# Causal attention on one core: projections as pairs of 64 columns in three PSUM banks, a new order of the unit, and 3 of 16 transfers issued by ScalarE

## The reference

```python
def _L0_attn_ref(x, qkv_w, qkv_b, out_w, out_b):        # x: (4, 1024, 128)
    qkv = jnp.einsum('bse,ehd->bshd', x, qkv_w) + qkv_b
    q, k, v = jnp.split(qkv, 3, axis=-1)
    logits = jnp.einsum('bqhd,bkhd->bhqk', q, k)
    logits = logits / jnp.sqrt(jnp.asarray(q.shape[-1], logits.dtype))
    mask = jnp.tril(jnp.ones((q.shape[1], q.shape[1]), dtype=jnp.bool_))
    logits = jnp.where(mask, logits, _large_negative_number(logits.dtype))
    probs = jax.nn.softmax(logits, axis=-1)
    attn = jnp.einsum('bhqk,bkhd->bqhd', probs, v)
    return jnp.einsum('bqhd,hde->bqe', attn, out_w) + out_b
...
x = x + _L0_attn_ref(xn, ...) + _L0_ffn_ref(xn, ...)     # layer 0
xn = _layernorm(x)
x = x + _L1_attn_ref(xn, ...) + _L1_ffn_ref(xn, ...)     # layer 1: fast weights, 8 experts
```

## Time and profile before

| | |
|---|---|
| time, median of 3 runs | 1467.65 us (1464.54 to 1470.5) |
| time of the profiled execution | 1468.25 us |
| its span, first to last instruction | 1466.5 us |
| mean granted TensorE clock | 0.997 |
| PE busy | 1414.2 us (96%) |
| DVE busy | 1254.1 us (86%) |
| POOL busy | 970.4 us (66%) |
| ACT busy | 917.8 us (63%) |
| attention of layer 0, unit 0 to unit 31 | from 64.93 us to about 920 us |

### The profile page before, as it was taken

One profiled execution on the slowest core, in us unless ns is written; L12 is line 12 of the kernel. 1 busy time (PEld: TensorE's weight loads), 2 busy tenths in 40 slices (PEclk: granted clock), 3 DMA queues, 4 the chain that ended last, 5 costly groups with the idle time before them and its releaser, 6 DMA issues.

```text
span 1466.5 us, 27229 instructions
## 1 busy us (share of the span) xinstructions
PE 1414.2 (96%) x9282; PEld 905.1 (62%) x9282; DVE 1254.1 (86%) x1966; ACT 917.8 (63%) x1862; POOL 970.4 (66%) x756
## 2 busy tenths in 40 slices
PE   8989999999999999999999998789999999999998
PEld 7756555555565565655655555456667676776767
DVE  7588888888888888888888877399999999999997
ACT  3456666766676666666666675557665675657552
POOL 5145545546555556555556554559999999999895
PEclk9999999999999999999999999999999999999999
DMA  8058777877787777777787778300000000000000
GB/s 191 1 130 213 180 175 174 194 169 177 174 190 182 173 176 187 172 185 178 180 190 170 171 182 202 86 1 1 1 8 8 1 8 1 8 8 1 8 1 15
DMA packets 77140, 163.98 MB, mean 112 GB/s; under 512 B 31410, under 2 KB 43724, under 8 KB 77004
## 3 DMA queue, kind: packets, MB, share of 16 engines
q1 hardware_dynamic: 77004, 162.24, 46.5%
HBM read 9.08 MB, written 2.10 MB: 8 GB/s over the span
## 4 chain that ended last, share of the span: by engine, by line
PE 83%; DVE 7%; issue 4%; POOL 3%; ACT 2%; DVEq 0%; ACTq 0%; POOLq 0%
PE accum L1096 18%; PE both L1031 13%; PE misc L998 9%; PE both L2786 8%; PE flips_all L1031 6%; PE flips_all L2809 4%; PE flips_all L1120 4%; PE misc L1008 4%; PE flips_all L2798 3%; PE flips_all L2846 2%; PE accum L2798 2%; PE accum L2809 2%; PE flips_all L2832 1%; ACT big L534 1%; PE flips_all L969 1%
## 5 line engine op out<-in xcount | busy, mean ns | idle before, releaser
L453 POOL TENSOR_SCALAR big<-big,recip 128x384 f32<-128x384 f32 (+7 forms) x512 | 376.1, 749 | 414.8 <-DVE recip L705 414.8
L713 DVE STREAM_TRANSPOSE big<-big 128x896 f32<-128x896 f32 (+7 forms) x288 | 346.0, 1228 | 17.5 <-POOL big L453 17.2
L534 ACT ACTIVATE big<-both,neg_max 128x1024 f32<-128x1024 f32 (+3 forms) x256 | 243.3, 956 | 169.0 <-DVE neg_max L695 160.5
L1096 PE MATMUL accum<-across,v_sb 128*64 128x256 f32 (+1 forms) x2560 | 271.6, 363 | 11.0 <-issue 10.9
L1096 PEld LDWEIGHTS accum<-across,v_sb 128*64 128x64 f32 x2560 | 178.8, 137 | 132.7 <-issue 68.9
L695 DVE TENSOR_REDUCE neg_max<-both 128x1 f32<-128x1024 f32 (+3 forms) x256 | 248.3, 1011 | 7.8 <-PE both L1036 7.8
L1031 PE MATMUL both<-qk_sb 64*128 64x512 f32 (+3 forms) x1024 | 212.9, 532 | 12.5 <-issue 8.6
L2786 PE MATMUL both<-slow_sb,h_T 128*128 128x512 f32 x384 | 181.1, 599 | 7.9 <-DVE xnT L2299 4.4
L1595 POOL TENSOR_TENSOR prod<-xnT,qs 128x1024 f32<-128x1024 f32 (+3 forms) x32 | 180.2, 5635 | 11.1 <-DVE qs L2299 11.1
L534 ACT ACTIVATE big<-flips_all,neg_max 128x128 f32<-128x128 f32 (+3 forms) x256 | 131.9, 526 | 83.3 <-DVE neg_max L695 46.9
L1031 PEld LDWEIGHTS both<-qk_sb 64*128 64x128 f32 x1024 | 93.9, 186 | 117.5 <-issue 117.5
(11 more groups left out here) (224 smaller groups left out, 2403.7 us busy)
## 6 DMA issues: line engine op xcount, KB each, us to landing
across<-big SPq DMA_DIRECT2D x1024, 144.0 KB, 2.5
out<-x SPq DMA_DIRECT2D x8, 256.0 KB, 2.3
x<-in_L_attn_x SPq DMA_DIRECT2D x3, 512.0 KB, 5.6
slow_sb<-in_L_attn_w_slow SPq DMA_DIRECT2D x3, 512.0 KB, 7.2
w_qk<-in_L_attn_qkv_w SPq DMA_DIRECT2D x2, 512.0 KB, 6.5
xn<-in_L_ffn_W SPq DMA_DIRECT2D x1, 1024.0 KB
x<-in_L_attn_x SPq DMA_DIRECT2D x2, 256.0 KB, 3.0
qs<-in_L_attn_qkv_w SPq DMA_DIRECT2D x1, 512.0 KB, 6.1
```

What stands on the lines that cost most here:

```text
L453: pool.tensor_scalar(part, part, recip[:, u % 2, SLOTS.index(row), h:h + 1], 0.0, ALU.mult, ALU.add).then_inc(scaled, 1)
L534: last = act.activation(probs_of(row, h).rearrange("p b j k -> p j b k"), scores_of(row, h).rearrange("p (j b k) -> p j b k", b=MOVES, k=3 ...
L713: dve.transpose(part, part).then_inc(turned[group_of(row)], 1)
L1096: last = pe.matmul(dst, lhsT=values_of(u, j, h), rhs=keys_of(g, rows[n:n + 2], j, h), start=j == 0, stop=j == rows[n + 1])
```

## The change

- `project`, `project_values` and `join` write their 128 output partitions as two matmuls of 64 stationary columns each (h = 0, 1), one to each half of the array's columns, with the same moving data.
- The projections of a unit take all three banks: (1, 0) and values 1 bank 0, (0, 0) bank 1, the others bank 2. Units 0 and the flips at the end stay in bank 2 (`FIRST`).
- ACT issues the last 3 of the 16 DMAs of each group (`move_rest`), SP the first 13 (`OWN`), but for the last unit, where SP issues all. SP's pass u is now `move(u - 1, 0)`, `move(u - 1, 1)`.
- `weigh` takes parts (pair of rows, from, to), so a group is weighed in other portions.
- PE, DVE, ACT and POOL have new orders of the unit. On DVE the turns of rows 3, 2 and 4 stand in the next pass, ahead of row 7's maxima, and the maxima of row 5 stand ahead of the turns of rows 1, 6 and 0.
- The tail into layer 1 follows these orders.

```diff
+LAST_LOW = 0, 0
-BANK = {('v', 0): 2, ('qk', 0, 1): 2, ('qk', 1, 0): 2, ('qk', 0, 0): 2, ('qk', 1, 1): 2, ('o', 0): 0, ('o', 1): 1, ('v', 1): 2}
+BANK = {('qk', 1, 0): 0, ('qk', 0, 1): 2, ('v', 1): 0, ('qk', 1, 1): 2, ('qk', 0, 0): 1, ('v', 0): 2, ('o', 0): 0, ('o', 1): 1}
+FIRST = ('v', 0), ('qk', 0, 1), ('qk', 1, 0), ('qk', 0, 0), ('qk', 1, 1), ('v', 1)
+BLOCKS = [(a, a ^ k) for k in range(MOVES) for a in (0, 2, 1, 3)]
+OWN = 13
...
         @block.sync   (move)
-                for k in range(MOVES):
-                    for a in (0, 2, 1, 3):
-                        b = a ^ k
-                        sp.dma_start(across[g][32 * b:32 * (b + 1), a, :], runs[g][32 * a:32 * (a + 1), b, :]).then_inc(moved[g], 16)
+                for a, b in BLOCKS[:OWN if u < UNITS - 1 else len(BLOCKS)]:
+                    sp.dma_start(across[g][32 * b:32 * (b + 1), a, :], runs[g][32 * a:32 * (a + 1), b, :]).then_inc(moved[g], 16)
...
+                move(u - 1, 0)
                 move(u - 1, 1)
-                move(u, 0)
...
         @block.gpsimd   (unit)
                 scale(u, 7, 0)
-                scale(u, 0, 1)
+                scale(u, 7, 1)
                 scale(u, 1, 0)
-                scale(u, 7, 1)
-                scale(u, 0, 0)
-                scale(u, 1, 1)
-                scale(u, 6, 0)
                 scale(u, 6, 1)
...
+                scale(u, 1, 1)
+                scale(u, 0, 0)
+                scale(u, 6, 0)
+                scale(u, 0, 1)
...
         @block.scalar
+            def move_rest(u, g):
+                if not 0 <= u < UNITS - 1:
+                    return
+                act.wait_ge(turned[g], TURNS[g] * (u + 1))
+                if u:
+                    act.wait_ge(weighed, weighed_at(u - 1, "high", g))
+                else:
+                    act.wait_ge(branch_ready, 2 * B)
+                for a, b in BLOCKS[OWN:]:
+                    act.dma_start(across[g][32 * b:32 * (b + 1), a, :], runs[g][32 * a:32 * (a + 1), b, :]).then_inc(moved[g], 16)
...
             def unit(u):
+                keep_part(u + 1, 1, 0)
                 softmax(u, 7, 1)
                 softmax(u, 7, 0)
                 if UNITS - B <= u < UNITS - 1:
                     first_norms(u - (UNITS - B))
+                move_rest(u - 1, 1)
+                softmax(u, 1, 1)
+                softmax(u, 1, 0)
                 softmax(u, 0, 1)
                 softmax(u, 0, 0)
-                softmax(u, 1, 1)
-                softmax(u, 1, 0)
-                keep_values(u + 1, 0)
+                softmax(u, 6, 1)
                 softmax(u, 6, 0)
                 keep_part(u + 1, 0, 1)
-                softmax(u, 6, 1)
-                keep_part(u + 1, 1, 0)
                 keep_att(u - 1, 0)
+                softmax(u, 2, 0)
                 softmax(u, 2, 1)
-                softmax(u, 2, 0)
+                softmax(u, 5, 1)
+                keep_values(u + 1, 1)
                 softmax(u, 5, 0)
-                softmax(u, 5, 1)
+                keep_part(u + 1, 1, 1)
+                softmax(u, 3, 0)
+                softmax(u, 3, 1)
+                softmax(u, 4, 0)
+                softmax(u, 4, 1)
                 keep_part(u + 1, 0, 0)
                 keep_att(u - 1, 1)
-                softmax(u, 3, 0)
-                softmax(u, 3, 1)
-                keep_part(u + 1, 1, 1)
-                softmax(u, 4, 0)
-                softmax(u, 4, 1)
-                keep_values(u + 1, 1)
                 keep_join(u - 1, 0)
+                move_rest(u, 0)
+                keep_values(u + 1, 0)
                 keep_join(u - 1, 1)
...
         @block.vector   (unit)
+                turn(u - 2, 3)
+                turn(u - 2, 2)
+                turn(u - 2, 4)
                 maximum(u - 1, 7, 1)
                 maximum(u - 1, 7, 0)
-                maximum(u - 1, 0)
                 maximum(u - 1, 1)
                 invert(u - 1, 0)
-                invert(u - 1, 4)
+                maximum(u - 1, 0)
+                maximum(u - 1, 6, 1)
                 maximum(u - 1, 6, 0)
-                maximum(u - 1, 6, 1)
...
                 turn(u - 1, 7)
                 invert(u - 1, 1)
+                invert(u - 1, 4)
                 maximum(u - 1, 2)
-                turn(u - 1, 0)
-                turn(u - 1, 1)
-                turn(u - 1, 6, 0)
-                turn(u - 1, 6, 1)
-                invert(u - 1, 6)
+                maximum(u - 1, 5, 1)
                 maximum(u - 1, 5, 0)
-                maximum(u - 1, 5, 1)
...
-                turn(u - 1, 2)
+                turn(u - 1, 1)
+                turn(u - 1, 6, 1)
+                turn(u - 1, 6, 0)
+                turn(u - 1, 0)
                 invert(u - 1, 2)
                 maximum(u - 1, 3)
+                invert(u - 1, 6)
...
                 turn(u - 1, 5)
                 invert(u - 1, 3)
-                turn(u - 1, 3)
-                turn(u - 1, 4)
...
         @block.tensor   (project; project_values and join in the same way)
-                pe.matmul(pool_of[k], lhsT=w_qk[:, c, P * n:P * (n + 1)], rhs=xnT[:, u // PAIRS, 512 * half:512 * (half + 1)],
-                          start=True, stop=True).then_inc(bank_made[k], 1)
+                for h in range(2):
+                    at = P * n + D * h
+                    last = pe.matmul(pool_of[k][D * h:D * (h + 1), :], lhsT=w_qk[:, c, at:at + D],
+                                     rhs=xnT[:, u // PAIRS, 512 * half:512 * (half + 1)], start=True, stop=True)
+                last.then_inc(bank_made[k], 1)
...
             def unit(u):
                 score(u, 0)
+                project(u + 1, 1, 0)
+                project(u + 1, 0, 1)
+                weigh(u - 1, 0, (0, 0, 2), (2, 0, 2))
                 score_small(u, 4)
-                project_values(u + 1, 0)
-                weigh(u - 1, 0, 0, 4)
                 score(u, 1)
+                weigh(u - 1, 0, (2, 2, 8))
                 score_small(u, 6)
-                project(u + 1, 0, 1)
-                weigh(u - 1, 0, 4, 8)
-                project(u + 1, 1, 0)
                 score(u, 2)
-                project(u + 1, 0, 0)
-                weigh(u - 1, 1, 0, 4)
-                weigh(u - 1, 1, 4, 6)
+                weigh(u - 1, 1, (0, 0, 4))
+                project_values(u + 1, 1)
+                project(u + 1, 1, 1)
                 score_small(u, 5)
                 score(u, 3)
-                project(u + 1, 1, 1)
+                weigh(u - 1, 1, (2, 0, 6))
+                project(u + 1, 0, 0)
+                project_values(u + 1, 0)
                 join(u - 1, 0)
                 join(u - 1, 1)
-                project_values(u + 1, 1)
```

More of the change, by code:

```diff
@@ L122, with __init__ @@
 GROUPS = (0, 1)
-EARLY = (('qk', 0, 1), ('qk', 1, 0))
+EARLY = (('qk', 1, 0), ('qk', 1, 1))
 class Tally:
[L128 to L132, removed]
+    def __init__(self, order, head=None, tail=None, over=()):
+        self.at, n = {}, 0
+        for body in range(-1, UNITS + 2):
+            if body == -1 and head is not None:
+                keys = [(key, 1) for key in head]
+            elif body >= UNITS and tail is not None:
+                keys = [(key, -1) for key in tail]
+            else:
+                keys = order
+            for key, ahead in keys:
+                if 0 <= body + ahead < UNITS:
                     n += 1
                     self.at[(body + ahead,) + key] = n
-        self.met = 0
+            for key in over if body == UNITS - 1 else ():
+                n += 1
+                self.at[(UNITS,) + key] = n
+        self.met, self.total = 0, n
     def __call__(self, u, *key):
@@ L208, in layer0 @@
                 ((0,), -1), ((1,), -1),
-            ])
+            ], tail=((0,), (1,)))
     tails = {}
@@ L1007, in project_values @@
                 for r in range(2):
-                    last = pe.matmul(pool_of[k][:, 256 * r:256 * (r + 1)], lhsT=xnT[:, b, P * (2 * c + r):P * (2 * c + r + 1)],
-                                     rhs=w_v[:, P * n:P * (n + 2)], start=True, stop=True)
+                    for h in range(2):
+                        at = P * (2 * c + r) + D * h
+                        last = pe.matmul(pool_of[k][D * h:D * (h + 1), 256 * r:256 * (r + 1)], lhsT=xnT[:, b, at:at + D],
+                                         rhs=w_v[:, P * n:P * (n + 2)], start=True, stop=True)
                 last.then_inc(bank_made[k], 1)
@@ L1079, in has_values, with weigh @@
                     pe.wait_ge(bank_kept[k], use)
[L1081 removed]
+            def weigh(u, g, *parts):
                 if done(u):
@@ L1088, in weigh @@
                     has_values(u, 0)
-                if hi > GB:
+                if parts[-1][2] > GB:
                     has_values(u, 1)
-                for n in range(0, GB, 2):
-                    for j in range(lo, min(hi, rows[n + 1] + 1)):
+                for n, lo, hi in parts:
+                    for j in range(lo, hi):
```

(8 more changed lines are left out.)

86 lines of the change are left out of this document (43 added, 43 removed).

## The result

The changed kernel takes 1553.53 us (median of 4 runs, 1550.79 to 1554.86) beside 1467.48 for the kernel before: a ratio of 1.0581, with a 95% interval from 1.0559 to 1.0602. The forecast was 1443.5 us with a range up to 1472; the time is 82 us beyond that end. The profiled execution has a span of 1553.1 us beside 1466.5.

What follows compares the result with a forecast made beforehand. PE bound the kernel at 26.61 us a unit; the loop over group 0 would set 25.65. Thirty units save 28.8 us, the last pays 4.3: 1468.25 becomes 1443.7, stated as 1443.5; own range 1433 to 1457, wider range 1425 to 1472.

Steps and rivals of the forecast that it cites:

- D = 11.25: Time in us from a group being turned to its copies' landing, foretold down from a mean of 12.5.
- part 2: ACT issues 3 of a group's 16 transfers: shorter landing, for 3.8 us of ACT's time a unit.
- both bounds of the split: Landing time 10.55 us if DMA engines take two trains at once (chance 0.18), about 12.0 if they are full (0.12).
- SP's train of 13: SP's 13 issues of a group were to take 8.3 us; stretching trains at DMA share 0.96 would show the forecast wrong.
- The slower rival: ACT's late issues queue behind SP's train, landing stays 12.5 us: 1481 us; with the case of costlier ACT issues, chance 0.15.
- The loop over group 0: Rows 0, 1, 6, 7: maxima and turns 10.0 us, landing, then weighing and scores 4.4; 25.65 us, setting the unit.
- PE's work: Per unit, 26.04 us falls to 25.1 through the pairs of 64 columns; bounds 25.0 and 26.0.
- A change of shape: Each change of PE's tile shape costs 0.19 us; four fewer a unit save 0.76 us.
- ACT's issues: Each issue costs ACT 0.64 us, 3.8 us a unit; at 1.3 us each a unit would take 27.3.
- wait ahead of row 5's scores: PE waits 0.1 to 0.2 us there for row 6's exponentials; this wait would show ACT's issues as the cause.
- POOL's 14.4 us: GpSimd's scaling and adding in a unit, taken only to follow the other engines.
- The last unit: Group 0 of unit 30 goes out behind W2 and b2; costs 4.3 us on the path into layer 1.

Runs made afterwards that it cites:

- a_early0: The changed kernel, with ACT issuing group 0's last three copies ahead of row 3's exponentials instead of behind the output projection's copy: 1505.42 us, ratio 1.0266.
- a_sp16: The changed kernel, but SP issues all 16 copies of a group and ACT none: 1529.88 us, ratio 1.0403.
- b_pairs: The kernel before with only the pairs of 64 columns in project, project_values and join; orders, banks and DMAs as before: 1466.9 us, ratio 0.9982.
- a_dev_w2: The changed kernel, with second_deviation behind group 0's scalings on POOL and unit 30's group 0 sent before W2 and b2: 1530.2 us, ratio 1.0414.
- b_pairs_act4: The kernel before in its own order, with the pairs and ACT issuing 4 of a group's 16 copies: 1479.19 us, ratio 1.0066.
- a_max5: The changed kernel, but DVE takes row 5's maxima behind the turns of rows 1, 6 and 0: 1629.25 us, ratio 1.1094.

## Why the prediction was wrong

**The step that failed** is D = 11.25 in part 2, the time from the turned group to its landing. It measured 13.65 and 12.66 us in the units shown and 13.2 on the mean. The prediction named both bounds of the split, 10.55 and 12.0, and chose a point near the lower one "since a landing only 1.94 us behind the last issue leaves no room for a pile of transfers". The half-size copies refute that reason: with the same issues and half the bytes D fell to 10.7, so the bytes held the landing, and no pile showed before since the issues came no faster than the copies drained. The copies of one group are 16 x 147,456 bytes, 10.3 us at the 228 GB/s of the earlier trace rows, and SP's train of 16 took 10.25: the two limits coincided before, so a train's shape couldn't tell which one held. The DMA share of 0.96 in the earlier trace rows could, and I discounted it. The Trainium skill ("DMA: Bandwidth & Descriptors", "Issuing engines are not separate DMA queues") says that a second issuer saves sequencer time alone; the runs agree: where both issue, the engines move 211 GB/s, and 242 in a train of SP's alone (windows in the last section), and in the order of before the split shortened D by 0.3 us. SP's train of 13 takes 9.4 us on the mean of the units, not 8.3: the prediction's own sign of being wrong.

**Why D became even longer than before.** The slower rival had part of the mechanism: ACT comes to group 0's three issues only when SP's train is nearly over. The timeline has them 6.3 us behind SP's first, and a_early0 shows their place to be worth 48 us. The rival took D = 12.5, as if late issues merely saved nothing; a_sp16, with the same order and SP alone, has 12.8, so 0.4 of the 13.2 are the late issues'. The other 0.4 over the 12.4 of before are there without ACT, in longer trains of SP (10.9 us beside 10.4); why they are longer stays open. That late issues cost time fits an overlap of the two trains: group 1's first copy, issued at 532.21, lands at 535.61, ahead of group 0's last, which is SP's own thirteenth (issued at 530.30, landed at 536.08). In the ten of 29 units where a copy of group 1 is ahead like that D is 13.6 on the mean, and 13.0 in the others. So the overlap is at most a part, and it is argued from the timeline; no run kept group 1's train back.

**Right in mechanism, nearly in size.** The loop over group 0, 14.4 + D, measured 14.5 + D. PE's work, 25.1 foretold, is 25.4 in the chain of the kernel after and 25.3 with the waits gone: inside the bounds, but 0.6 to 0.7 us saved and not 0.94. A change of shape costs 0.15 us in these rows, not 0.19. In the chain of the kernel after `project` and `project_values` take 0.86 beside others and 1.01 behind scores, and the output projection 1.75 instead of 1.97. The saving existed; at D = 13 nobody could use it. ACT's issues take 0.63 us each (three in 1.88), as assumed, and no wait ahead of row 5's scores appeared.

**Terms that the sum lacked.** `second_deviation` in the loop over group 0: I had read POOL's 14.4 us as following, and priced no instruction that the diff moved among its scalings. The last unit costs 11.9 us and not 4.3. Of the 7.6 us between, 2.8 are the later first issue (964.18 - 935.35 = 28.8, not 26.0, as the unit ahead is longer), 2.2 are D twice (12.6 and 13.4, not 11.25 and 12.5), and 2.5 PE's slow restart behind the wait. The loop over group 1 got no sum: in the kernel before it already took 26.3 us (13.8 from landing to first issue at the least, and 12.4), as long as PE's own work, which is what b_pairs ran into. And PE's granted clock, below.

**The sums.** With D = 13.2 the loop, 14.6 us from landing to first issue by the trace, gives 27.8 a unit, 30 x 1.2 = 36 of the 69.9 us lost. The trace divides the rest. From group 0's landing to the next first issue 15 of 30 units take 14.6 us. Eight take 16.2: there PE's clock fell behind the wait, 13 us in all. The six around the three ends of batches take 16.1 to 19.9, 21 us in all. The thirtieth, 21.5, belongs to the last unit above. The price of the change without the split, 60 us in a_sp16, is the largest single item. By the same count 24 of them are its D (14.6 + 12.8 = 27.4 a unit); the deviation and the last unit were shown in a_dev_w2 (23 us together), the maxima in the loop were not, and how much each is of the 60 was not measured.

## What to carry to other kernels

When a train of transfers is as long as its issues and also as long as its bytes at the measured rate, take the DMA share inside the train as the verdict: at 0.96, a second issuer took 0.3 us off 12.4 at best. Before an order spends the cover of a loop, price the loop at the measured latency and not at a hoped-for one: this order needed D under 12.3 us to break even by the prediction's own sum, and D had been 12.5. If transfers are shared out over two engines, those of the second must be early in the train, and nothing urgent may stand behind them: at its end they made D longer (13.2 beside 12.8 without them), and a fourth one, early, cost PE 18 us of waits.

## What the runs showed of the hardware

An issue of SP takes 0.59 us in the median of the kernel before, but single ones stretch to 1.97, and they do so with SP alone at work: 19 of some 1020 take over 1.2 us there. The 1.57 us of b_pairs_act4 stand at 504.52, 3 us before ACT's first issue. One such row of the kernel before, at a DMA share of 0.49:

```profile
494.91 1.53 SPq L355 DMA_DIRECT2D across<-big  x1
```

What stretches these is not shown. Beside that, issues of two engines that overlap are slower: in the kernel after those of SP that overlap one of ACT take 0.77 us on the mean, with half of the bytes 0.69, where SP alone in the kernel before has 0.61. The rate doesn't rise with two issuers. Windows of the kernel after, inside a train of SP's alone and where both issue (last: clock, DMA share, GB/s):

```profile
524.00:526.00 2.00, 2.00 (x24) 1.42 (x22) 1.94 (x4) 2.00 (x7) 2.00 (x4) 1.00 1.03 242
529.00:531.00 2.00, 2.00 (x20) 1.12 (x18) 1.58 (x2) 0.61 (x2) 1.27 (x1) 1.00 0.93 211
```

A wait of PE can be paid for twice. Behind the wait of 2.72 us the 16 records of the weighing took 1.73 us; behind one of 3.56 us they took 3.26, and the granted clock falls in that stretch. The length of the wait alone doesn't decide it: behind 2.19 us they took 2.45 (clock 0.75 from 506.50 to 508.00), and behind 2.83 us, at 157.76, they took 1.73 at the full clock. What decides it these rows don't tell.

```profile
97.64 3.56 issue
101.19 3.26 PE accum L1124 x16
...
504.19 2.19 issue
506.39 2.45 PE accum L1124 x16
```
```profile
358.00:366.00 8.00, 5.14 (x38) 3.18 (x40) 0.69 (x3) 2.30 (x4) 0.00 (x0) 0.79 1.00 237
```

The last row is the same event in unit 10, behind a wait of 3.57 us: a mean clock of 0.79 between full, 2.4 GHz, and half, 1.2 GHz. Over the stretch of all units the granted clock is 0.98 where it was 1.00, so of the 896 us at most some 2%, 18 us (an estimate from the two clocks), is lost that way; the eight loops of 16.2 us instead of 14.6 are 13 of them. In a_max5 the clock is 0.94.
